# A decoder layer on one core: the place of four statistics and of the next batch's preparation

## The chip, the core and the metric

The kernel runs on 1 core of one Trainium2 chip. The metric is the device time of one execution in microseconds. Engines are named as in the profile: PE is TensorE (PEld its weight loads), DVE is VectorE, ACT is ScalarE, POOL is GpSimd, SP is SyncE. A name with a q (ACTq, SPq) is the engine's queue, which also issues DMAs.

## The reference

A post-norm decoder layer over 4 batches of 512 tokens with 512 features:

```
x = layernorm(x + linear_attention(x))               # 16 heads, chunks of 64
x = layernorm(x + expert(x, w1, w2))                 # two int8-quantised linears with a SiLU gate between
x = layernorm(x + ffn(x))

ffn:    logits = x @ gate_w.T;  top 2 of 8 experts, softmax over the two logits
        h1_e = x @ w1.T + 2 * (x @ A1_e.T) @ B1_e.T  # w1, w3: 1408 x 512; rank 16
        h3_e = x @ w3.T + 2 * (x @ A3_e.T) @ B3_e.T
        act  = silu(h1_e) * h3_e
        out  = sum over the two chosen experts of
               weight_e * (act @ w2.T + 2 * (act @ A2_e.T) @ B2_e.T)
```

float32 products are made of three matmuls of split operands (hi x hi, lo x hi, hi x lo).

## The kernel before

The first phase does attention for all batches and the expert of batch 0. The second phase (`mixture`), where the change lies, runs the feed-forward part of batch b and, beside it, the expert of batch b + 1. Each engine has its own hand-written program; they meet through semaphores only. `batches` gives the order on each: `prepare(0)`, then `hidden(b)` and `between(b)` for b = 0 and 1 in a hardware loop, then for b = 2, and for b = 3 without an expert (there is no next batch). I call the end of `hidden(b)` with `between(b)` and the start of the next `hidden` turn b; there are turns 0, 1 and 2 with an expert.

`hidden(b)` goes over 11 tiles f of 128 of the 1408 hidden features. Per tile PE forms h1 and h3 with the first choice's adapter (`first(b, f, 0)` and `first(b, f, 1)`), then adds the difference to the second choice's adapter (`second`, matmuls of L2172). ScalarE takes silu of h1 for each choice (`silu_out`, L1710). VectorE multiplies by the routing weight (`weighted`, L1905) and by h3 (`activation`, L1913), adds the two choices (L2080) and makes the low parts (`activation_lo`, L1895 and L1898) of what ScalarE has rounded (`activation_hi`). `second(b, f, 1)` overwrites h3, so it waits for `activation(b, f, 0)`. PE's `adapters_both(b, f)` follows and signals z_done.

Beside tile 10, the expert's output lies ready as a residual sum in `tokens`. VectorE takes its bn_stats (`expert_statistics`, four of L2022) before `weighted(b, 10, 0)`, and combines them (`expert_variance`, six small operations, L115 to L120) before `weighted(b, 10, 1)`.

`between(b)` has PE multiply the activations by w2: `whole_down(b, f)` for f = 0 to 8, each 4 x 3 matmuls into four banks, then tiles 9 and 10 with `adapters_out` per 128 tokens. Among these stands the preparation of batch b + 1: transposes of the tokens (`x_transposed`, L2233), `logits_across`, `logits_by_token`, `adapters_in` for U1 and U3, `masks_transposed` and `weights_spread`. A down tile comes through ScalarE's queue: `fetch_down` issues its load of 256 KB, `split_down` waits for the landing and rounds it (L1555), GpSimd's `split_down` forms the low part (L1505), and the slot is loaded again; three slots go round. `next_down(b, f)` is the split of tile f and the fetch of tile f + 2. Between them, in ScalarE's order, stand `expert_deviation` (a square root, L1674), `expert_normalise` (L1679), the store of the tokens (`store_x2`), `z_split`, `x_hi` (L1565), `masks_out` (L1580) and others. The transposes wait for the normalised tokens.

SyncE's queue loads the up weights (`f_up`, 1408 KB a tile): tile 0 of the next batch once z_done of tile 9 has come, then x3.

VectorE in `between(b)`: the shift of the expert's norm (`expert_shift`), `mask_z`, `z_split`, `x_lo`, `choose` and `weigh` (the top 2), `mask_adapters` (L1864, waits for `masks_out`), `adapters_lo`, in turns 0 and 1 `channel_top` of the expert after (L1933, two reductions over 2048 elements), and `normalise`: the residual sum of PE's outputs, its bn_stats, and the norm (L2101 to L2112). Then `hidden(b + 1)` begins on it.

Of the kernel before, what the change touches and what calls it, by code (L numbers as in the profile page):

```python
# [1246 lines left out]
def mixture(nc, shared, used, x1_dram, x2_dram, up_dram, w1, w2, down_stream, descending, out_dram):  # L1247
# [9 lines left out]
    with ExitStack() as ctx:  # L1257
# [169 lines left out]
        def tiles(b, f):  # L1427
            return b * FT + f + 1
# [114 lines left out]
        def _(sc):  # L1543
# [7 lines left out]
            def split_down(b, f):  # L1551
                r = f % DOWNS
                sc.wait_ge(down_loaded[r], PRIMED + 16 * (b * PER[r] + f // DOWNS + 1))
                sc.wait_ge(down_done, PRIMED + (tiles(b, f - DOWNS) if f >= DOWNS else b * FT))
                sc.activation(down_hi[:, r, :], down_raw[:, r, :], ACT.Copy).then_inc(down_hi_ready, 1)  # L1555

            def next_down(b, f):
                split_down(b, f)
                if f + DOWNS - 1 < FT:
                    fetch_down(b, f + DOWNS - 1)  # L1560
# [32 lines left out]
            def z_split(b):  # L1593
                sc.wait_ge(z_summed, PRIMED + b + 1)
                sc.activation(z_hi[:, :], zm[:, 2, :], ACT.Copy).then_inc(z_hi_ready, 1)
# [157 lines left out]
            def between(b, expert, another):  # L1753
                for f in range(DOWNS, 2 * DOWNS - 1):
                    fetch_down(b, f)
                if expert:
                    expert_deviation(b)
                next_down(b, 3)
                if expert:
                    expert_normalise(b)  # L1760
                    store_x2(b)
                next_down(b, 4)
                z_split(b)
                if expert:
                    x_hi(b + 1, 0)
                    x_hi(b + 1, 1)
                next_down(b, 5)
                if expert:
                    x_hi(b + 1, 2)
                    x_hi(b + 1, 3)  # L1770
                    logits_out(b + 1)
                next_down(b, 6)
                if expert:
                    softmax_exp(b + 1)
                    masks_out(b + 1)
                next_down(b, 7)
                if expert:
                    masked_hi(b + 1, 0)
                    masked_hi(b + 1, 1)
                next_down(b, 8)  # L1780
                if expert:
                    masked_hi(b + 1, 2)
                    masked_hi(b + 1, 3)
                    weights_out(b + 1)
                next_down(b, 9)
                next_down(b, 10)
                if another:
                    root(b + 1, 0)
                deviation(b)
# [4 lines left out]
        def _(dve):  # L1794
# [224 lines left out]
            def expert_statistics(b):  # L2019
                for t in range(TT):  # L2020
                    dve.wait_ge(summed, PRIMED + b * TT + t + 1)
                    dve.bn_stats(e_stats[:, t, :], xe[:, t, :]).then_inc(e_stats_ready, 1)  # L2022

            def expert_variance(b):
                dve.wait_ge(e_stats_ready, PRIMED + b * TT + TT)
                moments(dve, e_stats, e_part, e_mean[:, :], e_rstd[:, 0, :], waiter(e_moment_ready, b * 2))\
                    .then_inc(e_var_ready, 1)

            def expert_shift(b):
                dve.wait_ge(e_std_ready, PRIMED + b + 1)  # L2030
                dve.reciprocal(e_rstd[:, 2, :], e_rstd[:, 1, :]).then_inc(e_rstd_ready, 1)
                dve.wait_ge(e_rstd_ready, PRIMED + 2 * b + 1)
                dve.scalar_tensor_tensor(e_mean[:, :], e_mean[:, :], -1.0, e_rstd[:, 2, :],
                                         ALU.mult, ALU.mult).then_inc(e_rstd_ready, 1)

            def hidden(b, expert):
                for item in (WB0, WB1):
                    k, n = slot(b, item)
                    dve.wait_ge(drained[k], PRIMED + n + 1)
                for f in range(FT):  # L2040
                    if expert and f == 1:
                        scale_tokens(b, 0)
                        row_scale(b, 0, 0)
                    if expert and f == 2:
                        round_w(b, 0)
                    if expert and f == 5:
                        linear_out(b, 0)
                    if expert and f == 6:
                        channel_ratio(b, 1)
                    if expert and f == 7:  # L2050
                        scale_tokens(b, 1)
                        row_scale(b, 1, 0)
                    if expert and f == 8:
                        clamp_x(b, 1)
                    if expert and f == 10:
                        expert_statistics(b)
                    weighted(b, f, 0)
                    activation(b, f, 0)
                    if expert and f == 1:
                        row_scale(b, 0, 1)  # L2060
                    if expert and f == 2:
                        clamp_x(b, 0)
                    if expert and f == 4:
                        channel_top(b, 1, 1)
                    if expert and f == 5:
                        expert_activation(b)
                        channel_top(b, 1, 0)
                    if expert and f == 6:
                        channel_scale(b, 1)
                    if expert and f == 7:  # L2070
                        row_scale(b, 1, 1)
                        round_w(b, 1)
                    if expert and f == 9:
                        linear_out(b, 1)
                    if expert and f == 10:
                        expert_variance(b)
                    weighted(b, f, 1)
                    activation(b, f, 1)
                    dve.wait_ge(act_ready, PRIMED + 2 * tiles(b, f))
                    dve.tensor_tensor(act[:, 2, :], act[:, 0, :], act[:, 1, :], ALU.add).then_inc(sum_ready, 1)  # L2080
                    activation_lo(b, f)
# [34 lines left out]

            def between(b, expert, another):
                if expert:
                    expert_shift(b)
                mask_z(b)  # L2120
                z_split(b)
                if expert:
                    for c in range(KT):
                        x_lo(b + 1, c)
                    choose(b + 1)
                    weigh(b + 1)
                    mask_adapters(b + 1)
                    adapters_lo(b + 1)
                if another:
                    for i in range(2):  # L2130
                        channel_top(b + 1, 0, i)
                normalise(b, expert, another)
# [4 lines left out]
        def _(pe):  # L2137
# [75 lines left out]
            def whole_down(b, f):  # L2213
                for t in range(TT):
                    down(b, f, t)
# [197 lines left out]
            def between(b, expert, another):  # L2413
                whole_down(b, 0)
                whole_down(b, 1)
                adapters_second(b, FT - 1)
                adapters_both(b, FT - 1)
                whole_down(b, 2)
                if expert:
                    x_transposed(b + 1, 0)  # L2420
                    x_transposed(b + 1, 1)
                whole_down(b, 3)
                if expert:
                    x_transposed(b + 1, 2)
                    x_transposed(b + 1, 3)
                down(b, 4, 0)
                down(b, 4, 1)
                if expert:
                    logits_across(b + 1)
                down(b, 4, 2)  # L2430
                down(b, 4, 3)
                if expert:
                    logits_by_token(b + 1)
                    adapters_in(b + 1, U1)
                whole_down(b, 5)
                if expert:
                    adapters_in(b + 1, U3)
                if expert:
                    masks_transposed(b + 1)
                whole_down(b, 6)  # L2440
                if expert:
                    weights_spread(b + 1)
                whole_down(b, 7)
                whole_down(b, 8)
                for t in range(TT):
                    down(b, FT - 2, t)
                    down(b, FT - 1, t)
                    adapters_out(b, t)
                if another:
                    first_maxima(b + 1)  # L2450
# [92 lines left out]
```

## Time and profile before

| | us |
|---|---|
| three runs | 1130.33, 1132.45, 1132.54; median 1132.45 |
| profiled execution | 1128.95 |
| its span | 1127.1 |
| PE, DVE, ACT, POOL busy | 1030.8, 717.8, 402.7, 295.3 |
| mean granted clock of TensorE | 0.977 |

The span goes from the first to the last instruction. The profiled execution's own time is 1.85 us above its span. A clock of 1.00 is 2.4 GHz, 0.50 is 1.2 GHz. Recorded matmul durations overlap: from start to start a matmul of 512 columns takes less than the 0.40 us that its row shows.

### The profile page before, as it was taken

To read this page: it belongs to the slowest core of one execution; us is meant where nothing else is said; L and a number is where in the kernel's file an instruction comes from. 1 tells how busy PE (TensorE), PEld (TensorE's weight loads), DVE (VectorE), ACT (ScalarE), POOL (GpSimd) and SP (SyncE) were. 2 spreads that over 40 slices of the span, in tenths; PEclk is the share of its full clock that TensorE was granted. 3 is DMA by queue.
4 is the path that set the end of the run, shared out by engine and by line. 5 is a ranking of instruction groups with operands and counts; after the bars stand their busy time and mean duration, and the time that the engine had idled before them with its cause. 6 is when DMAs were issued, how large, how long until landed. Compare 5 with 4: busy or idle time off the path is not lost.

```text
span 1127.1 us, 13755 instructions
## 1 busy us (share of the span) xinstructions
PE 1030.8 (91%) x4920; PEld 809.6 (72%) x4920; DVE 717.8 (64%) x1150; ACT 402.7 (36%) x623; POOL 295.3 (26%) x245
## 2 busy tenths in 40 slices
PE   3799999989999827999999899999999999999997
PEld 2577777767777625777768687777777877888885
DVE  4565786785576646957657867764976774554542
ACT  3234333323342233344443253434253434322231
POOL 2247674543224400201222200142110132200021
PEclk9899999999999968999999999999999999999999
DMA  7116664130021025243463152446143327134421
GB/s 261 62 61 232 214 232 146 61 104 10 10 92 31 1 78 225 99 161 111 163 219 123 39 210 103 170 158 233 39 158 134 133 79 276 57 140 154 172 66 56
DMA packets 47862, 142.98 MB, mean 127 GB/s; under 512 B 3497, under 2 KB 14633, under 8 KB 42161
## 3 DMA queue, kind: packets, MB, share of 16 engines
q1 hardware_dynamic: 28720, 118.71, 28.8%
q10 hardware_dynamic: 19072, 23.35, 6.4%
q8 instruction: 42, 0.69, 0.3%
q14 instruction: 28, 0.22, 0.1%
HBM read 114.66 MB, written 27.39 MB: 126 GB/s over the span
## 4 chain that ended last, share of the span: by engine, by line
PE 44%; DVE 13%; issue 3%; ACT 2%; POOL 1%; DMA 1%; DVEq 0%; ACTq 0%
PE f_h L106 7%; PE f_h L107 7%; PE f_h L108 7%; PE f_h L2172 4%; PE f_y L106 3%; PE f_y L107 3%; PE f_y L108 3%; DVE f_q_mem L1933 2%; DVE f_work L1913 1%; PE f_y L2362 1%; DVE f_work L1905 1%; PE f_z_sum L106 1%; PE f_z_sum L108 1%; PE f_z_sum L107 1%; PE f_z_second L107 1%
## 5 line engine op out<-in xcount | busy, mean ns | idle before, releaser
L106 PE MATMUL f_h<-f_xT_hi,f_up 128*128 128x512 f32 x352 | 140.5, 399 | 1.6 <-issue 0.9
L107 PE MATMUL f_h<-f_xT_hi,f_up 128*128 128x512 f32 x352 | 138.4, 393 | 0.0
L108 PE MATMUL f_h<-f_xT_lo,f_up 128*128 128x512 f32 x352 | 137.7, 391 | 0.0
L106 PE MATMUL ring<-w_hi,xT_hi 128*128 128x512 f32 x256 | 110.4, 431 | 24.4 <-POOL xT_lo L429 21.8
L1505 POOL TENSOR_TENSOR f_down_lo<-f_down_raw,f_down_hi 128x512 fp32r<-128x512 f32 x44 | 61.1, 1390 | 227.5 <-ACT f_down_hi L1555 227.5
L1710 ACT ACTIVATE f_work<-f_h 128x512 f32<-128x512 f32 x88 | 52.4, 596 | 171.4 <-PE f_h L2172 114.8
L1905 DVE TENSOR_TENSOR f_work<-f_work,f_weightT 128x512 f32<-128x512 f32 x88 | 65.1, 739 | 73.7 <-ACT f_work L1710 69.9
L1516 POOL TENSOR_TENSOR weights<-weights,f_rows 128x512 f32<-128x512 f32 (+1 forms) x24 | 31.9, 1360 | 299.9 <-ACT f_rows L1637 183.6
L1913 DVE TENSOR_TENSOR f_work<-f_h,f_work 128x512 f32<-128x512 f32 x88 | 60.8, 691 | 70.8 <-PE f_h L108 65.3
L107 PE MATMUL ring<-w_hi,xT_lo 128*128 128x512 f32 x256 | 103.7, 405 | 0.0
L108 PE MATMUL ring<-w_lo,xT_hi 128*128 128x512 f32 x256 | 103.5, 404 | 0.0
L443 POOL TENSOR_TENSOR rot_b<-qk,ropes 128x256 f32<-128x256 f32 x64 | 55.8, 893 | 101.2 <-ACT qk L548 101.2
L106 PEld LDWEIGHTS ring<-w_hi,xT_hi 128*128 128x128 f32 x256 | 49.4, 193 | 41.8 <-POOL xT_lo L429 23.6
L106 PEld LDWEIGHTS f_h<-f_xT_hi,f_up 128*128 128x128 f32 x352 | 66.6, 189 | 16.9 <-issue 2.0
L108 PEld LDWEIGHTS f_h<-f_xT_lo,f_up 128*128 128x128 f32 x352 | 66.4, 189 | 14.8
L107 PEld LDWEIGHTS f_h<-f_xT_hi,f_up 128*128 128x128 f32 x352 | 66.5, 189 | 14.2
L106 PE MATMUL f_y<-f_down_hi,f_both_hi 128*128 128x512 f32 x176 | 71.9, 409 | 0.0
L107 PE MATMUL f_y<-f_down_hi,f_both_lo 128*128 128x512 f32 x176 | 70.6, 401 | 0.0
L108 PE MATMUL f_y<-f_down_lo,f_both_hi 128*128 128x512 f32 x176 | 70.5, 401 | 0.0
L2172 PE MATMUL f_h<-f_umT_hi,f_up 128*128 128x512 f32 x176 | 57.6, 408 | 13.9 <-DVE f_work L1913 13.9
L1604 ACT ACTIVATE f_second_hi<-f_work 128x512 fp32r<-128x512 f32 x44 | 27.9, 635 | 109.0 <-DVE f_work L1913 109.0
L108 PEld LDWEIGHTS ring<-w_lo,xT_hi 128*128 128x128 f32 x256 | 49.8, 195 | 12.2
(306 smaller groups left out, 2244.0 us busy)
## 6 DMA issues: line engine op xcount, KB each, us to landing
f_up<-up_scratch SPq DMA_DIRECT2D x44, 1408.0 KB, 6.2
f_down_raw<-in_down_stream ACTq DMA_DIRECT2D x44, 256.0 KB, 3.6
f_x<-x_scratch SPq DMA_DIRECT2D x7, 1024.0 KB, 8.8
scaled_w<-in_up_stream SPq DMA_DIRECT2D x6, 704.0 KB, 5.4
up_scratch<-q_mem SPq DMA_DIRECT2D x6, 704.0 KB, 3.6
up_scratch<-scaled_w SPq DMA_DIRECT2D x6, 704.0 KB, 3.1
x_tok<-in_x SPq DMA_DIRECT2D x4, 1024.0 KB, 5.6
out<-f_x SPq DMA_DIRECT2D x8, 512.0 KB, 3.1
```

What stands on the lines that cost most here:

```text
L106: pe.matmul(out, lhs_hi, rhs_hi, start=start, stop=False)
L107: pe.matmul(out, lhs_lo, rhs_hi, start=False, stop=False)
L108: return pe.matmul(out, lhs_hi, rhs_lo, start=False, stop=stop)
L443: pool.tensor_tensor(b4[:, :, :, two], q4[:, :, :, 1 - two], sin[:, :, two].unsqueeze(1).to_broadcast([P, H, DK // 2]), ALU.mult).then_inc ...
L1505: pool.tensor_tensor(down_lo[:, f % DOWNS, :], down_raw[:, f % DOWNS, :], down_hi[:, f % DOWNS, :].bitcast(F32), ALU.subtract).then_inc(do ...
L1516: pool.tensor_tensor(we[:, t, 0:C], we[:, t, 0:C], rows[:, 1, 0:C], ALU.mult).then_inc(w_scaled, 1)
L1604: sc.activation(second_hi[:, :], act[:, 1, :], ACT.Copy).then_inc(act_hi_ready, 1)
L1710: sc.activation(silu[:, choice, :], h_ps[0][:, :], ACT.Silu).then_inc(silu_ready, 1)
L1905: dve.tensor_tensor(silu[:, choice, :], silu[:, choice, :], weightT[:, choice, :], ALU.mult)\
L1913: dve.tensor_tensor(act[:, choice, :], h_ps[1][:, :], silu[:, choice, :], ALU.mult)\
L1933: dve.tensor_reduce(top[:, i, 0:C], (xe, we)[i][:, :, 0:C].rearrange("p t c -> p c t"), AX.X, ALU.max, apply_absolute_value=True).then_inc ...
L2172: last = pe.matmul(h_ps[i][:, :], weights(f, l, cols), r[:, rhs, :], start=False, stop=True, skip_group_check=True)
```

## The change

On VectorE, `expert_statistics` moves from before `weighted(b, 10, 0)` to behind `activation(b, 10, 0)`, and `expert_variance` from there to the start of `between`. On PE and ScalarE each part of the next batch's preparation moves behind one more down tile. No operation is added or taken away.

```
 ScalarE, between:
                 next_down(b, 4)
                 z_split(b)
+                next_down(b, 5)
                 if expert:
                     x_hi(b + 1, 0)
                     x_hi(b + 1, 1)
-                next_down(b, 5)
+                next_down(b, 6)
                 if expert:
                     x_hi(b + 1, 2)
                     x_hi(b + 1, 3)
                     logits_out(b + 1)
-                next_down(b, 6)
+                next_down(b, 7)
                 if expert:
                     softmax_exp(b + 1)
                     masks_out(b + 1)
-                next_down(b, 7)
+                next_down(b, 8)
                 if expert:
                     masked_hi(b + 1, 0)
                     masked_hi(b + 1, 1)
-                next_down(b, 8)
+                next_down(b, 9)
                 if expert:
                     masked_hi(b + 1, 2)
                     masked_hi(b + 1, 3)
                     weights_out(b + 1)
-                next_down(b, 9)
                 next_down(b, 10)
 VectorE, hidden:
-                    if expert and f == 10:
-                        expert_statistics(b)
                     weighted(b, f, 0)
                     activation(b, f, 0)
...
                     if expert and f == 10:
-                        expert_variance(b)
+                        expert_statistics(b)
                     weighted(b, f, 1)
                     activation(b, f, 1)
 VectorE, between:
                 if expert:
+                    expert_variance(b)
                     expert_shift(b)
 PE, between:
                 whole_down(b, 2)
+                whole_down(b, 3)
                 if expert:
                     x_transposed(b + 1, 0)
                     x_transposed(b + 1, 1)
-                whole_down(b, 3)
+                whole_down(b, 4)
                 if expert:
                     x_transposed(b + 1, 2)
                     x_transposed(b + 1, 3)
-                down(b, 4, 0)
-                down(b, 4, 1)
+                down(b, 5, 0)
+                down(b, 5, 1)
                 if expert:
                     logits_across(b + 1)
-                down(b, 4, 2)
-                down(b, 4, 3)
+                down(b, 5, 2)
+                down(b, 5, 3)
                 if expert:
                     logits_by_token(b + 1)
                     adapters_in(b + 1, U1)
-                whole_down(b, 5)
+                whole_down(b, 6)
                 if expert:
                     adapters_in(b + 1, U3)
-                if expert:
                     masks_transposed(b + 1)
-                whole_down(b, 6)
+                whole_down(b, 7)
                 if expert:
                     weights_spread(b + 1)
-                whole_down(b, 7)
                 whole_down(b, 8)
```

## Rows read from the trace of the kernel before

**Rows 1.** The page's first part: busy time, share of the span, instructions.

```profile
PE 1030.8 (91%) x4920; PEld 809.6 (72%) x4920; DVE 717.8 (64%) x1150; ACT 402.7 (36%) x623; POOL 295.3 (26%) x245
```

**Rows 2.** The chain that ended last, turn 1: start, us on the chain, engine, line.

```profile
746.04 1.86 DVE f_e_stats L2022 x3
...
783.19 1.03 ACT f_maskT L1580
```

**Rows 3.** Timeline of PE: start, us, operation, [idle before it <- who ended it].

```profile
568.17 0.74 PE L2172 MATMUL f_h<-f_umT_hi,f_up 128*128 128x512 f32 x2 [2.41 <-DVE f_work L1913]
...
633.62 0.73 PE L2172 MATMUL f_h<-f_umT_hi,f_up 128*128 128x512 f32 x2 [3.37 <-DVE f_work L1913]
...
749.26 0.73 PE L2172 MATMUL f_h<-f_umT_hi,f_up 128*128 128x512 f32 x2 [2.39 <-DVE f_work L1913]
...
811.07 0.74 PE L2172 MATMUL f_h<-f_umT_hi,f_up 128*128 128x512 f32 x2 [0.91 <-DVE f_work L1913]
...
925.98 0.73 PE L2172 MATMUL f_h<-f_umT_hi,f_up 128*128 128x512 f32 x2 [2.47 <-DVE f_work L1913]
...
938.71 1.09 PE L2233 MATMUL f_h<-ident,tokens 128*128 128x128 f32 x8 [1.26 <-ACT tokens L1679]
```

**Rows 4.** Timeline of PE: the first matmul behind down tile 1, turns 1 and 2.

```profile
757.90 0.40 PE L106 MATMUL f_z_second<-f_second_hi,f_up 128*128 128x512 f32 x1
...
933.09 0.39 PE L106 MATMUL f_z_second<-f_second_hi,f_up 128*128 128x512 f32 x1
```

**Rows 5.** Windows: length, busy PE, PEld, DVE, ACT, POOL, granted clock, DMA share, GB/s.

```profile
634.00:636.00 2.00, 2.00 (x11) 1.90 (x10) 1.38 (x3) 0.53 (x1) 0.00 (x0) 0.60 0.05 8
...
751.00:752.00 1.00, 1.00 (x4) 0.78 (x3) 0.97 (x3) 0.63 (x1) 0.00 (x0) 0.50 0.00 0
```

**Rows 6.** Timeline of DVE around the statistics of turn 1.

```profile
743.73 1.78 DVE L1898 TENSOR_TENSOR f_both_lo<-f_work,f_both_hi 128x512 fp32r<-128x512 f32 x1
745.43 2.46 DVE L2022 BATCH_NORM_STATS2 f_e_stats<-tokens 128x6 f32<-128x512 f32 x4
...
749.13 0.16 DVE L115 TENSOR_TENSOR f_e_part<-f_e_stats 128x8 f32<-128x8 f32 x1
...
749.83 0.69 DVE L1905 TENSOR_TENSOR f_work<-f_work,f_weightT 128x512 f32<-128x512 f32 x1
```

**Rows 7.** Timeline of POOL in turn 1: the low parts of down tiles 1 and 4.

```profile
744.93 1.74 POOL L1505 TENSOR_TENSOR f_down_lo<-f_down_raw,f_down_hi 128x512 fp32r<-128x512 f32 x1
...
763.51 1.30 POOL L1505 TENSOR_TENSOR f_down_lo<-f_down_raw,f_down_hi 128x512 fp32r<-128x512 f32 x1 [2.85 <-ACT f_down_hi L1555]
```

**Rows 8.** Timeline of ACT in turn 1: down tiles 3 and 4, x_hi(2) with x_hi(3).

```profile
758.66 0.63 ACT L1555 ACTIVATE f_down_hi<-f_down_raw 128x512 fp32r<-128x512 f32 x1 [3.88 <-DMA f_down_raw<-in_down_stream]
...
762.80 0.63 ACT L1555 ACTIVATE f_down_hi<-f_down_raw 128x512 fp32r<-128x512 f32 x1 [0.68 <-PE f_y L108]
...
766.72 1.18 ACT L1565 ACTIVATE f_xT_hi<-f_h 128x512 fp32r<-128x512 f32 x2 [1.28 <-PE f_h L2233]
```

**Rows 9.** DMA issues: up tile 0; down tiles 3, 6: KB each, us to landing.

```profile
f_up<-up_scratch SPq DMA_DIRECT2D x1, 1408.0 KB, 6.2
...
f_down_raw<-in_down_stream ACTq DMA_DIRECT2D x1, 256.0 KB, 6.4
...
f_down_raw<-in_down_stream ACTq DMA_DIRECT2D x1, 256.0 KB, 5.2
```

**Rows 10.** Timeline of SP's queue, turn 1: the issue of up tile 0.

```profile
751.25 0.32 SPq L1441 DMA_DIRECT2D f_up<-up_scratch  x1
```

**Rows 11.** Timeline of PE, turn 1: the first matmul of the logits.

```profile
768.69 0.40 PE L106 MATMUL f_h<-f_xT_hi,f_a_hi 128*8 128x512 f32 x1
```

**Rows 12.** Timeline of DVE: the ends of turns 1 and 2.

```profile
784.25 0.69 DVE L1864 TENSOR_TENSOR f_work<-f_z_sum,f_maskT 128x512 f32<-128x512 f32 x1 [5.53 <-ACT f_maskT L1580]
...
807.07 0.18 DVE L2110 RECIPROCAL f_rstd<-f_rstd 128x4 f32<-128x4 f32 x1 [0.27 <-ACT f_rstd L1599]
...
971.98 0.69 DVE L2101 TENSOR_TENSOR f_x<-f_y,f_x 128x512 f32<-128x512 f32 x1 [4.26 <-PE f_y L108]
```

More of the change, by code:

```diff
@@ L1763, in between @@
                 z_split(b)
+                next_down(b, 5)
                 if expert:
@@ L1766, in between @@
                     x_hi(b + 1, 1)
-                next_down(b, 5)
+                next_down(b, 6)
                 if expert:
@@ L1771, in between @@
                     logits_out(b + 1)
-                next_down(b, 6)
+                next_down(b, 7)
                 if expert:
@@ L1775, in between @@
                     masks_out(b + 1)
-                next_down(b, 7)
+                next_down(b, 8)
                 if expert:
@@ L1779, in between @@
                     masked_hi(b + 1, 1)
-                next_down(b, 8)
+                next_down(b, 9)
                 if expert:
@@ L1784, in between @@
                     weights_out(b + 1)
-                next_down(b, 9)
                 next_down(b, 10)
@@ L2054, in hidden @@
                         clamp_x(b, 1)
-                    if expert and f == 10:
-                        expert_statistics(b)
                     weighted(b, f, 0)
@@ L2075, in hidden @@
                     if expert and f == 10:
-                        expert_variance(b)
+                        expert_statistics(b)
                     weighted(b, f, 1)
@@ L2118, in between @@
                 if expert:
+                    expert_variance(b)
                     expert_shift(b)
@@ L2418, in between @@
                 whole_down(b, 2)
+                whole_down(b, 3)
                 if expert:
@@ L2421, in between @@
                     x_transposed(b + 1, 1)
-                whole_down(b, 3)
+                whole_down(b, 4)
                 if expert:
@@ L2425, in between @@
                     x_transposed(b + 1, 3)
-                down(b, 4, 0)
-                down(b, 4, 1)
+                down(b, 5, 0)
+                down(b, 5, 1)
                 if expert:
                     logits_across(b + 1)
-                down(b, 4, 2)
-                down(b, 4, 3)
+                down(b, 5, 2)
+                down(b, 5, 3)
                 if expert:
@@ L2434, in between @@
                     adapters_in(b + 1, U1)
-                whole_down(b, 5)
+                whole_down(b, 6)
                 if expert:
                     adapters_in(b + 1, U3)
-                if expert:
                     masks_transposed(b + 1)
-                whole_down(b, 6)
+                whole_down(b, 7)
                 if expert:
                     weights_spread(b + 1)
-                whole_down(b, 7)
                 whole_down(b, 8)
```

## The prediction

> **What bounds the kernel now.** I began with the page: TensorE is busy for 91% of the span [rows 1], so a change of order can only win where TensorE stands still or runs at half clock, or lose by making it do so. Next came the chain of waits and the idle times of PE around the three turns from one batch to the next (turn 0 near 568 to 634 us, turn 1 near 749 to 811, turn 2 near 926 to 986). The reader should see two kinds of place on the chain: the four bn_stats of L2022, and, at the other end of a turn, the copy of the masks (L1580) followed by VectorE [rows 2]. In the idle times the same pattern stands in every turn [rows 3]: PE waits 2.41, 2.39 and 2.47 us for VectorE's product L1913 before `second(b, 10, 1)`; in turn 2 it waits 1.26 us more for ScalarE's normalised tokens before the transposes; and at the start of the next batch it waits for VectorE again, 3.37 us in turn 0, 0.91 in turn 1.
>
> The first wait costs more than its length in turn 1 (and in turn 0, whose wait is alike). The same 30 matmuls take 8.64 us from 749.26 to 757.90 in turn 1, and 7.11 from 925.98 to 933.09 in turn 2 [rows 3, 4]. The difference, 1.5 us, is a stretch at the lower level of TensorE's clock: 0.50 granted, 1.2 GHz, behind 2.4 us without a matmul [rows 5]. Turn 2's wait of 2.47 us was followed by no such stretch in this execution. One matmul at full clock is 7.11/30, about 0.235 us, a down tile of 12 is 2.8.
>
> **Who owns the end of a turn.** In turn 1 VectorE waits 5.53 us for the masks, starts at 784.25, and then has one idle time, 0.27 us before L2110, until it hands over L1913 just ahead of 811.07 [rows 3, 12]. Everything in between (masking, `channel_top`, the last norm of this batch, then `weighted` and `activation` of the next) is queued back to back. So in turns 0 and 1 the time of the whole turn is that of the masks plus a fixed 26.8 us (811.07 less 784.25); what PE gains before is waited away at its end. Turn 2 has no `channel_top`, and there VectorE waits 4.26 us for PE's outputs at 971.98 [rows 12]: PE's own position counts.
>
> **Part 1, statistics behind the first activation.** In turn 1 VectorE ends both_lo at 745.51 (743.73 + 1.78) and does the four bn_stats (2.46 us, some 2.4 from start to start) before L1905 [rows 6]. After, L1905 comes first. But GpSimd's second `split_down` stands from 744.93 to 746.67 [rows 7], and VectorE's operations with two SBUF inputs take longer beside it: L1898 1.78 us, against 0.69 for L1905 at 749.83 with GpSimd idle [rows 6]; the bn_stats, with one such input, are not lengthened. I let L1905 finish 0.6 us behind GpSimd, at 747.3, and L1913 at 748.0. PE starts at 748.05 instead of 749.26: 1.2 us gained, 1.15 us of idle time left. Behind the waits of 0.91 and 1.26 us no stretch at 0.50 stands in this trace, so I count the 1.5 us back in turns 0 and 1. Bounds of the gain in waiting: 1.2, and 2.4 if L1905 gets in at once.
>
> The Trainium skill, page "SBUF — State Buffer", section "Who interferes with whom", says that a VectorE instruction with two SBUF inputs and a GpSimd instruction that reads SBUF exclude each other, whoever issues first holding the ports for its whole length. GpSimd's row starts first here, which by that rule gives the 1.2; had VectorE been first, it would be 2.4.
>
> Behind it the statistics lie in front of `weighted(b, 10, 1)`. From 748.0 they take 2.4, so L1905 starts at 750.3 rather than 749.83 [rows 6]: 0.5 us late, although the six small variance operations (0.7 us, 749.13 to 749.83) have gone. Queued behind are activation, sum, both lows, and ScalarE's `activation_hi`, after which it issues the loads of down tiles 3 and 4: 0.5 us later each. PE itself has two down tiles to do before it wants these lows, 5.6 us of cover. `expert_variance` in `between` ends near 754.6, hidden by ScalarE's wait for down tile 3 until 758.66 [rows 8]; without that cover it would cost its 0.7 us.
>
> **Part 2, one down tile earlier than the preparation.** No instruction is added or removed on PE, ScalarE or the DMA queues; GpSimd's and SyncE's order stays. But the masks now stand behind one more down tile, +2.8 us, so the masks come earlier only if PE gained more than that. PE gained 2.7 in turns 0 and 1 (shift at best about +0.1) and 1.2 plus the 1.26 of the transposes in turn 2 (about +0.3).
>
> The real limit is another chain, from the landing L of down tile 3 (758.66 in turn 1 [rows 8]). ScalarE splits it, normalises, issues the store and gets to tile 4 at L + 4.14, as before; GpSimd has its low at L + 6.15 (763.51 + 1.30) [rows 7, 8]. PE now needs that low before tile 4, ahead of transposes 2 and 3: L + 6.15 + 2.8 + 0.95 + 1.4 = L + 11.3 for the logits matmuls. And ScalarE now splits tile 6 before x_hi(2). Tile 6 is fetched at L + 4.2 behind the 1 MB store and needs 5.2 us [rows 9]: L + 9.4. Half a microsecond of split, then the 1.97 us from x_hi(2) to the logits (766.72 to 768.69) [rows 8, 11]: L + 11.9. Before, the logits started at L + 10.0, right behind the down matmuls. So the masks shift by 1.85 plus the shift of L.
>
> L: `f_up` of 1408 KB is issued at 751.25 and needs 6.2 us, so it lands near 757.4; the 256 KB of down tile 3 need 6.4 and land 1.2 behind it [rows 8 to 10], so I read them as held up by it. `f_up` waits for z_done of tile 9, right behind the wait that shrinks, hence 1.2 us earlier. I take L 1.2 us earlier. Bounds: 0.5 later (its own issue) and 2.4 earlier. The masks then come 1.85 - 1.2 = 0.65 us later than now.
>
> The Trainium skill, page "DMA: Bandwidth & Descriptors", section "Queues, rings and completion order", says that each DMA engine goes round robin between queues, packet by packet. A tile on ScalarE's queue should then not stand behind SyncE's, and its landing would follow its own issue, 0.5 later, which is the slow rival below; the 6.4 us speak against an even share.
>
> **The sum.** Turn 0: +0.65. Turn 1: +0.65, and now PE arrives 2.15 earlier at the end of the turn (2.8 less 0.65), so its 0.91 us of waiting becomes 0.91 + 2.15 + 0.65 = 3.7 us, and behind 3.37 the clock fell in turn 0 [rows 5]: +1.5. Turn 2: 0.65 - 2.8 = -2.15, kept by PE. Together 3 x 0.65 + 1.5 - 2.8 = +0.65 us. The profiled execution took 1128.95 us (span 1127.1 and 1.85 around it), 3.5 less than the median of 1132.45; a difference carries over, so 1133.1. The last batch has no preparation behind it and changes nothing.
>
> **Rivals.** (a) The low clock in turn 1 stays away: -0.85, 1131.6. Speaks for it: turn 2's 2.47 us without one. (b) L1905 isn't held by GpSimd: PE's first wait closes, `f_up` starts 2.4 earlier, the masks shift by 1.85 - 2.4 = -0.55; 3 x -0.55 - 1.3 = -2.95, 1129.5. Against it: [rows 6, 7]. (c) Slower: down tile 3 lands 0.5 later, with its issue; shift 2.35, 3 x 2.35 - 1.3 = +5.75, 1138.2. It decides once the shift passes 1.2, that is, once L moves less than 0.65 forward. (d) VectorE doesn't set the end of turns 0 and 1, the shift reaches PE as in turn 2: 3 x -2.15 = -6.45, 1126.0. Against it: 26 us without a gap. (e) Turn 2's wait is followed by a low clock in most other executions, so that the runs win 1.5 there which this trace hides: -0.85, 1131.6.
>
> **Chances.** The forecast 45%, (a) and (e) 25% together, (b) 10%, (c) 13%, (d) 5%, 2% else. Changes under 0.2%, 2.3 us, can't be told from none. Forecast, (a) and (e) lie inside, with an error of about 1.5 us each, giving some 56% same; (b), (d) and the low tails 23% faster; (c) and the high tails 21% slower. The range runs from (b) to just short of (c): 1129.5 to 1137.5.
>
> **What will show it.** PE's wait before `second(b, 10, 1)` about 1.15 us and no 0.50 clock behind it; L1905 there 1.3 to 1.8 us long; down tile 3 landing about 1.2 us earlier against the wait's end kept in place; gaps of some tenths of a microsecond before down tiles 3 and 4 and the logits; VectorE's start on the masks 0.65 later within the turn; PE's wait at the end of turn 1 above 3 us with a 0.50 clock; turn 2 alone about 2 us shorter. I am wrong if the first wait closes, or the masks come earlier than now, or VectorE has idle time behind them.

## The result: slower by 0.46%, and where it went

The changed kernel takes 1137.1 us (median of 6 runs, 1135.36 to 1138.27) against 1132.38 for the kernel before (6 runs): ratio 1.0046, 95% interval 1.0033 to 1.0058. I had forecast 1133.1 and no measurable change. 1137.1 lies inside my range, 1129.5 to 1137.5, but only because the range ended just short of the slow rival (c), and (c) is what happened. The profiled execution took 1135.39 us, its span is 1133.6.

The page's first part, of the kernel after:

```profile
PE 1030.5 (91%) x4911; PEld 809.6 (71%) x4920; DVE 723.6 (64%) x1150; ACT 402.6 (36%) x623; POOL 297.1 (26%) x245
```

PE has the same work as in [rows 1] (nine matmul records are missing from this trace); the time is idle time. The timeline of PE after, at the places of [rows 3] and at new ones (start, us, operation, idle time before it and who ended it):

```profile
568.87 0.73 PE L2171 MATMUL f_h<-f_umT_hi,f_up 128*128 128x512 f32 x2 [1.13 <-DVE f_work L1913]
582.13 0.49 PE L106 MATMUL f_y<-f_down_hi,f_both_hi 128*128 128x512 f32 x1 [1.79 <-POOL f_down_lo L1505]
...
626.26 0.79 PE L106 MATMUL f_h<-f_xT_hi,f_up 128*128 128x512 f32 x1 [3.19 <-issue]
...
637.81 0.72 PE L2171 MATMUL f_h<-f_umT_hi,f_up 128*128 128x512 f32 x2 [2.16 <-DVE f_work L1913]
...
752.11 0.73 PE L2171 MATMUL f_h<-f_umT_hi,f_up 128*128 128x512 f32 x2 [1.14 <-DVE f_work L1913]
765.09 0.49 PE L106 MATMUL f_y<-f_down_hi,f_both_hi 128*128 128x512 f32 x1 [1.53 <-POOL f_down_lo L1505]
769.24 0.50 PE L106 MATMUL f_y<-f_down_hi,f_both_hi 128*128 128x512 f32 x1 [0.22 <-POOL f_down_lo L1505]
774.96 0.40 PE L106 MATMUL f_h<-f_xT_hi,f_a_hi 128*8 128x512 f32 x1 [0.40 <-DVE f_xT_lo L1810]
815.20 0.74 PE L2171 MATMUL f_h<-f_umT_hi,f_up 128*128 128x512 f32 x2 [2.28 <-ACT f_work L1710]
817.27 1.20 PE L2171 MATMUL f_h<-f_umT_hi,f_up 128*128 128x512 f32 x2 [1.10 <-DVE f_work L1913]
...
931.58 0.73 PE L2171 MATMUL f_h<-f_umT_hi,f_up 128*128 128x512 f32 x2 [1.21 <-DVE f_work L1913]
```

The first wait of each turn has fallen to 1.13 to 1.21 us, as worked out. New are the waits for the low part of down tile 3 (1.79, 1.53 and, in turn 2, 1.53 us), of tile 4 (0.22) and for the logits (0.40). At the end of turn 1 PE now waits 3.4 us (2.28 and 1.10) instead of 0.91, and at the end of turn 0 3.19 and 2.16 us instead of 0.88 and 3.37.

Executions differ by up to 4.4 us before the first turn, where all kernels here run the same code, so I compare lengths inside the second phase and not spans. The marks are rows of PE: the transposes of the quantised activations ahead of turn 0 (541.63 before, 543.61 after), the transposes of the channel maxima in the batch that follows (694.39 and 698.50; then 871.06 and 877.93), and the second-choice matmuls behind turn 2 (985.90 and 992.32). Differences of neighbours, and the start of the copy of the masks counted from the same mark ahead of turn 1 (722.73 and 726.84):

| | turn 0 | turn 1 | turn 2 | masks of turn 1 |
|---|---|---|---|---|
| before | 152.76 | 176.67 | 114.84 | 60.46 |
| after | 154.89 | 179.43 | 114.39 | 62.60 |
| difference | +2.13 | +2.76 | -0.45 | +2.14 |

The sum is +4.44 us; the other 2 us between the two spans arose before turn 0. Counted the same way, the masks come 2.37 us later in turn 0 and 2.35 in turn 2. The low clock behind the first wait of turn 1 is gone (1.00, where before there was 0.50 [rows 5]), and one has come at the end of the turn. In turn 0 the kernel before has two low stretches (from 569.5 and 634.4), the kernel after one (from 626.2, at the end of the wait of 3.19). Windows of the kernel after, columns as in [rows 5]:

```profile
753.00:755.00 2.00, 2.00 (x10) 1.60 (x9) 2.00 (x4) 0.00 (x0) 0.00 (x0) 1.00 0.32 56
...
817.00:819.00 2.00, 1.73 (x5) 1.45 (x6) 0.81 (x3) 0.00 (x0) 0.00 (x0) 0.58 0.60 226
```

Timelines of SyncE's and ScalarE's queues and of ScalarE after, and the issue of down tile 3 with its us to landing (the last line):

```profile
753.80 0.32 SPq L1441 DMA_DIRECT2D f_up<-up_scratch  x1
754.32 0.39 SPq L1445 DMA_DIRECT2D f_x<-x_scratch  x1
...
756.69 0.34 ACTq L1547 DMA_DIRECT2D f_down_raw<-in_down_stream  x1
...
763.06 0.63 ACT L1555 ACTIVATE f_down_hi<-f_down_raw 128x512 fp32r<-128x512 f32 x1 [3.15 <-DMA f_down_raw<-in_down_stream]
...
f_down_raw<-in_down_stream ACTq DMA_DIRECT2D x1, 256.0 KB, 6.3
```

From the mark, `f_up` is now issued 1.56 us earlier (26.96 instead of 28.52; [rows 10]), as the forecast wanted. But down tile 3 is split at 36.22 instead of 35.93 [rows 8]: 0.29 us later (0.50 in turn 0, 0.48 in turn 2). It did not move with `f_up`. And VectorE's queue behind the masks is as long as before, here its two idle times (timeline of DVE after; compare [rows 12]):

```profile
790.49 0.69 DVE L1864 TENSOR_TENSOR f_work<-f_z_sum,f_maskT 128x512 f32<-128x512 f32 x1 [5.51 <-ACT f_maskT L1580]
813.26 0.18 DVE L2108 RECIPROCAL f_rstd<-f_rstd 128x4 f32<-128x4 f32 x1 [0.27 <-ACT f_rstd L1599]
```

790.49 to 817.27 is 26.78 us, against 26.82 before. Turn 0 is different, which I had overlooked: there the stretch lasts 30.42 us before (603.20 to 633.62) and 30.26 after, because VectorE stands idle inside it. Timeline of DVE, the first product of the next batch, first in the kernel before, then after:

```profile
632.15 0.69 DVE L1905 TENSOR_TENSOR f_work<-f_work,f_weightT 128x512 f32<-128x512 f32 x1 [3.69 <-issue]
```

```profile
636.34 0.69 DVE L1905 TENSOR_TENSOR f_work<-f_work,f_weightT 128x512 f32<-128x512 f32 x1 [3.60 <-ACT f_work L1710]
```

In the kernel before, the silu that it reads had ended at 628.21. The same idle time of 3.56 to 3.69 us stands in every kernel here, and only at the end of turn 0, where the programs step back to the start of the hardware loop; at the end of turn 1, where they leave it, there is none (L1905 starts at 809.60, behind an operation that ends at 809.49). The DMA view of the kernel before lists two packets of kind instruction between 629 and 634 us and none between 803 and 812. That points to the loading of instructions, but no run here tests it.

### The profile page after: what moved, and what is told of

Same layout as the page of the kernel before. It is cut to its first block, busy times and chain, and to the rows that moved or that the text cites. A ratio compares the mean times of both kernels' runs of the same rounds, so it can differ in the third digit from the quotient of the medians.

```text
span 1133.6 us, 13746 instructions
## 1 busy us (share of the span) xinstructions
PE 1030.5 (91%) x4911; PEld 809.6 (71%) x4920; DVE 723.6 (64%) x1150; ACT 402.6 (36%) x623; POOL 297.1 (26%) x245
## 4 chain that ended last, share of the span: by engine, by line
PE 42%; DVE 12%; DMA 3%; issue 3%; ACT 3%; POOL 1%; ACTq 0%; DVEq 0%
PE f_h L106 7%; PE f_h L107 7%; PE f_h L108 7%; PE f_h L2171 4%; DMA f_down_raw<-in_down_stream 3%; PE f_y L106 2%; PE f_y L108 2%; PE f_y L107 2%; DVE f_work L1905 2%; DVE f_work L1913 1%; PE f_y L2361 1%; DVE f_q_mem L1933 1%; PE f_z_sum L106 1%; PE f_z_sum L107 1%; PE f_z_sum L108 1%
## 5 line engine op out<-in xcount | busy, mean ns | idle before, releaser
L1905 DVE TENSOR_TENSOR f_work<-f_work,f_weightT 128x512 f32<-128x512 f32 x88 | 69.2, 787 | 73.6 <-ACT f_work L1710 73.5
```

What stands on the lines that cost most here:

```text
L1905: dve.tensor_tensor(silu[:, choice, :], silu[:, choice, :], weightT[:, choice, :], ALU.mult)\
```

## The experiments

Each was run on the same chip as the kernel before, whose medians in the three groups were 1132.83, 1132.22 and 1132.92. Turn lengths come from the same marks.

**1 and 2: each part alone.** e1 has part 1 on the order of before, e2 part 2 with the statistics left in place; their diffs are the two halves of the diff shown.

> The order of before, with the statistics alone moved behind the first activation (and the variance into between). Theory T (the landing of down tile 3 paces a turn): PE's first wait falls from 2.4 to 1.15 us, but the load of tile 3 is issued 0.5 later and lands 0.3 to 0.5 later, and the transposes wait for it (normalised tokens at landing + 3.5), so PE idles some 3 us before them instead of 0 to 1.3. Each turn 0.3 to 0.5 longer, 1133.3 to 1134; up to 1.5 a turn more if that idle time brings the low clock. Rival R (PE's first wait is what costs): 1.2 us a turn gained and 1.5 of clock in turns 0 and 1, about 1126.

> The statistics and the variance where they were, the preparation one down tile later. Theory T: down tile 3 lands as in the kernel before; the masks come 2.4 us later in turns 0 and 1 and both turns lengthen by that, turn 2 shortens by about 0.9: 1136.4. Rival R (the later order is free and hides the 1.26 us before the transposes): 1131 to 1132.4.

e1: 1138.53 us, ratio 1.0038 (1.0024 to 1.0052). Turns 155.45, 177.16, 118.08. e2: 1136.7 us, ratio 1.0038 (1.0023 to 1.0052). Turns 153.86, 180.62, 114.83. Both parts lose alone, and together they lose about as much as either. PE of e1, timeline:

```profile
753.86 0.74 PE L2171 MATMUL f_h<-f_umT_hi,f_up 128*128 128x512 f32 x2 [1.13 <-DVE f_work L1913]
768.72 1.06 PE L2232 MATMUL f_h<-ident,tokens 128*128 128x128 f32 x8 [3.39 <-ACT tokens L1679]
...
945.69 1.97 PE L2232 MATMUL f_h<-ident,tokens 128*128 128x128 f32 x8 [3.17 <-ACT tokens L1679]
```

The wait taken away at 753.86 has gone to the transposes. From its mark (728.60) they stand at 40.12, against 39.64 in the kernel before: 0.48 us later, as much as the landing of down tile 3, whose load is issued 0.37 later (29.84 from the mark instead of 29.47). Turn 1 grew by 0.49. The rest of the loss goes with the low clock: from 944.7 on the record shows 6.8 us at 0.50 in turn 2, which is 3.2 us longer, and turn 0 (2.7 us longer) has a stretch behind its wait of 3.53 and one of 6.8 us at its end. Rival R (1126) falls. In e2 the load is issued as before (29.46 from the mark), but `f_up` only 0.52 us ahead of it instead of 0.95, and it lands 0.80 later; the masks of turn 1 come 2.65 us later than before and the turn is 3.95 longer, low clock at its end included. Turn 2 has a low stretch that the profile before lacks (from 934.7) and gains nothing instead of 0.9. T gave 1136.4.

**3: the loads beside down tile 3, held back.**

```
                     sp.wait_ge(z_done, PRIMED + tiles(b, FT - 2))
+                    sp.wait_ge(down_loaded[0], PRIMED + 16 * (b * len(range(0, FT, DOWNS)) + 2))
                     load_up(0)
```

> The changed kernel, in which SyncE's queue issues up tile 0 and x3 of the next batch only when down tile 3 has landed. If f_up and x3 on the other queue slow down tile 3, it lands 2.6 to 3.5 us behind its issue instead of 6.4, the waits for the lows of tiles 3 and 4 go, and the turns shorten by 0.9 to 2.5 each (tile 6 and the store now run beside f_up): 1130 to 1134.5. If the 6.4 us are not from sharing: 1137, tile 3 as late as now.

1144.64 us, ratio 1.0094 (1.0077 to 1.0112). DMA issues of down tiles 3 and 6 (us to landing), and ScalarE's timeline at tile 6:

```profile
f_down_raw<-in_down_stream ACTq DMA_DIRECT2D x1, 256.0 KB, 2.7
...
f_down_raw<-in_down_stream ACTq DMA_DIRECT2D x1, 256.0 KB, 10.3
...
779.17 0.63 ACT L1556 ACTIVATE f_down_hi<-f_down_raw 128x512 fp32r<-128x512 f32 x1 [5.38 <-DMA f_down_raw<-in_down_stream]
```

Half the expectation held: alone, down tile 3 lands 2.7 us behind its issue instead of 6.3, so the rest is sharing. The time was missed by 10 us, since the two loads now run beside the store and tiles 5 and 6. Tile 6 takes 10.3 us, x_hi(2) is queued behind its split in the new order, and PE waits 3.4 to 4.6 us before the logits. The place in ScalarE's order for which I had counted 0.6 us costs whatever that load costs.

**4: the split of tile 6 behind x_hi(3).**

```
-                next_down(b, 6)
                 if expert:
                     x_hi(b + 1, 2)
                     x_hi(b + 1, 3)
+                next_down(b, 6)
+                if expert:
                     logits_out(b + 1)
```

> The changed kernel with ScalarE's split of down tile 6 moved from before x_hi(2) to behind x_hi(3). Theory T: the wait of 0.38 to 0.45 us before the logits goes, the masks come 0.4 earlier in each turn: 1135.9. If the split of tile 6 is not what the logits wait for: 1137.1 and the wait stays.

1137.3 us, ratio 1.0033 (1.0021 to 1.0044); the changed kernel had 1.0046, so the times don't tell them apart. The wait before the logits fell from 0.38 and 0.40 to 0.18 us in turns 0 and 1: tile 6 was what they waited for, but it is worth 0.2 us and not the 0.4 expected. This execution had two low stretches more (766.8 in turn 1, 947.7 in turn 2) and a longer one at the end of turn 1 (818.0), which cover anything of that size.

**5 and 9: the two loads behind the transposes.** On e1. e5 moves both, e9 only x3.

```
-                    sp.wait_ge(z_done, PRIMED + tiles(b, FT - 2))
-                    load_up(0)
-                    sp.wait_ge(summed, PRIMED + TT * (b + 1))
-                    load_x3(x2_dram[bass.ts(b, T), :])
                     tokens_transposed(b + 1)
                     if another:
                         sp.wait_ge(x2_stored, PRIMED + 16 * (b + 2))
                         load_expert_tokens(b + 1)
+                    sp.wait_ge(z_done, PRIMED + tiles(b, FT - 2))
+                    load_up(0)
+                    sp.wait_ge(summed, PRIMED + TT * (b + 1))
+                    load_x3(x2_dram[bass.ts(b, T), :])
```

> The statistics moved, the preparation where it was, and SyncE's loads of up tile 0 and of x3 for the next batch issued behind the transposes and the expert's tokens. If the landing of down tile 3 beside those two loads is what paces a turn: it lands 2.7 us behind its issue, the wait of 3.2 to 3.5 us before the transposes (statistics alone) goes, the masks come 2.7 us earlier than in the kernel before, and every turn is some 2.5 us shorter: 1125 to 1128. If it isn't: as the statistics alone, 1138.

> Statistics moved, preparation where it was; of SyncE's two loads only x3 is issued late (behind the transposes), up tile 0 stays early. Theory X (down tile 3 shares the DMA engines with f_up and then with x3, and lands only when x3 has nearly landed): without x3 it lands 3 to 4.5 us behind its issue, PE's wait before the transposes falls from 3.3 to about 1 or less, 1124 to 1127. The reading of the prediction (down tile 3 is held by f_up alone): x3 makes no difference, still 6.3 us, 1138.

e5: 1122.89 us, 2 us below the range expected, ratio 0.9916 (0.9903 to 0.9929); turns 149.66, 173.75, 112.09; the wait before the transposes is gone in every turn. e9: 1124.7 us, ratio 0.9937 (0.9919 to 0.9954); turns 150.11, 174.38, 112.73. Down tile 3 of e5 (us to landing); then of e9 `f_up`, down tile 3 and PE's wait for the tokens in turn 1:

```profile
f_down_raw<-in_down_stream ACTq DMA_DIRECT2D x1, 256.0 KB, 2.6
```

```profile
f_up<-up_scratch SPq DMA_DIRECT2D x1, 1408.0 KB, 6.0
...
f_down_raw<-in_down_stream ACTq DMA_DIRECT2D x1, 256.0 KB, 3.8
...
759.05 1.06 PE L2232 MATMUL f_h<-ident,tokens 128*128 128x128 f32 x8 [0.60 <-ACT tokens L1679]
```

With `f_up` still early, the load of 256 KB takes 3.8 us, with both loads early 6.5 (e1). Of the 3.9 us that the two loads add to the 2.6 of e5, the larger part, 2.7, comes from x3, 1 MB behind `f_up` on the same queue.

**6 and 7: who owns the end of a turn.** The two reductions of `channel_top` move ahead of the masks, on the kernel after (e6) and before (e7). The second line keeps the transposes of the maxima waiting for both.

```
                     for c in range(KT):
                         x_lo(b + 1, c)
+                    if another:
+                        channel_top(b + 1, 0, 1)
                     choose(b + 1)
                     weigh(b + 1)
+                    if another:
+                        channel_top(b + 1, 0, 0)
                     mask_adapters(b + 1)
                     adapters_lo(b + 1)
-                if another:
-                    for i in range(2):
-                        channel_top(b + 1, 0, i)
...
-                    pe.wait_ge(top_ready, PRIMED + 4 * b + i + 1)
+                    pe.wait_ge(top_ready, PRIMED + 4 * b + 2)
```

> The changed kernel with the two reductions of channel_top (7.6 us of VectorE) moved into idle times of VectorE ahead of the masks. Theory V (VectorE's queue behind the masks sets the end of turns 0 and 1): PE's waits at the end of both turns go and PE's own position counts, turn 0 about 5 us shorter than in the kernel before, turn 1 about 1, turn 2 as in the changed kernel: 1125 to 1127. Rival d of the prediction (VectorE does not set the end): 1137 as the changed kernel.

> The kernel before with the same move of channel_top. Theory V: turn 0 4.9 us shorter (3.4 of wait, 1.5 of clock), turn 1 0.75, turn 2 the same: 1127. Against it the changed kernel with this move should then be about 1 us faster instead of 4.7 slower, since its 0.5 to 0.6 us a turn of PE position is no longer lost. Rival d: 1132.8.

e6: 1129.13 us, ratio 0.9966 (0.9954 to 0.9979); turns 151.16, 176.67, 115.76. e7: 1131.38 us, ratio 0.9986 (0.9976 to 0.9997); turns 151.75, 176.27, 116.06. DVE and PE of e6, timelines; then DVE of e7 at the end of turn 0:

```profile
796.17 0.69 DVE L2099 TENSOR_TENSOR f_x<-f_y,f_x 128x512 f32<-128x512 f32 x1 [1.37 <-PE f_y L108]
...
810.99 0.73 PE L2172 MATMUL f_h<-f_umT_hi,f_up 128*128 128x512 f32 x2 [0.16 <-DVE f_work L1913]
```

```profile
633.93 0.69 DVE L1905 TENSOR_TENSOR f_work<-f_work,f_weightT 128x512 f32<-128x512 f32 x1 [3.59 <-ACT f_work L1710]
```

V holds in kind: VectorE now waits for PE, PE's 3.4 us at the end of turn 1 have become 0.16 (with 1.40 us at 823.47, a tile later), and the changed kernel goes from 0.46% slower to 0.34% faster than before, although its masks come 2.70 us late. Once that queue is gone the change no longer costs: e6 lies 2 us under e7, with intervals that overlap by 0.0003. V's sizes were too large: I had counted turn 0 at 4.9 to 5 us, and it gave 1.0 (e7) and 1.6 (e6). VectorE's idle time at the loop's step is still there in both, so PE still waits behind it: 2.52 us in e7, with a low stretch behind, 2.12 in e6, with none.

**8 and 12: the causes taken away together.** e8 is e5 with the move of `channel_top`. e12 adds one wait on GpSimd, before its second split of a batch with an expert.

```
                 for f in range(DOWNS):
+                    if expert and f == 1:
+                        pool.wait_ge(act_ready, PRIMED + 2 * tiles(b, FT - 1) - 1)
                     split_down(b, f)
```

> Statistics moved, preparation where it was, up tile 0 and x3 loaded late, channel_top in VectorE's idle times. Both causes removed: turn 0 shorter by 7, turn 1 by 3.4, turn 2 by 2.5: 1119 to 1121. If the late loads and the end of a turn overlap in what they win, 1124.

> The fastest kernel so far (statistics moved, both loads late, channel_top in idle times), and GpSimd waits for the activation of tile 10's first choice before its second split. If GpSimd's split is what makes L1905 take 1.8 us there, L1905 takes 0.7, PE's wait of 1.13 us before the second-choice matmuls goes, and each turn is 1.1 us shorter: 1117.3. If L1905 is long for another reason, 1120.7 and the wait stays.

e8: 1120.72 us, ratio 0.9896 (0.9883 to 0.9910); turns 147.97, 173.86, 112.06. e12: 1116.89 us, ratio 0.9874 (0.9855 to 0.9894); turns 146.80, 172.02, 110.98. L1905 in front of the statistics, timelines of DVE: first the kernel after, then e12 with the bn_stats behind it.

```profile
749.54 1.79 DVE L1905 TENSOR_TENSOR f_work<-f_work,f_weightT 128x512 f32<-128x512 f32 x1
```

```profile
741.17 0.68 DVE L1907 TENSOR_TENSOR f_work<-f_work,f_weightT 128x512 f32<-128x512 f32 x1
...
742.49 2.46 DVE L2024 BATCH_NORM_STATS2 f_e_stats<-tokens 128x6 f32<-128x512 f32 x4
```

1.79 us beside GpSimd, 0.68 without it, and PE's wait before the second-choice matmuls no longer appears: the forecast of part 1 by GpSimd's rows was right, and every turn is 1.1 to 1.8 us shorter than in e8. This is what the Trainium skill, page "SBUF — State Buffer", section "Who interferes with whom", says of VectorE instructions with two SBUF inputs beside GpSimd.

**10 and 11: late loads with the whole change, and alone.** The diff of e5 on the kernel after and on the kernel before.

> The whole change with both loads late. With down tile 3 early the masks are limited by PE alone: one down tile more (2.8) against the 1.2 and 1.5 gained, so the masks come as in the kernel before and 2.5 later than without the later preparation. Turns 0 and 1 unchanged to the kernel before, turn 2 2.5 shorter: 1130. If the later preparation costs nothing where down tile 3 is early: 1123.

> The kernel before with both loads late and nothing else. There down tile 3 lands early too, but PE reaches the transposes only 0.1 us before the tokens are ready in turns 0 and 1, so nothing is won there; turn 2 loses its 1.26 us of waiting: 1131. If the loads are worth more by themselves than that, the 9 us of the two together belong mostly to them: 1125.

e10: 1127.98 us, ratio 0.9963 (0.9954 to 0.9972); turns 151.50, 177.94, 112.01. e11: 1129.12 us, ratio 0.9968 (0.9954 to 0.9982); turns 152.03, 175.47, 114.86. Both came 2 us below their figures. Late loads win 0.32% alone and the moved statistics lose 0.38% alone, but the two together win 0.84%: the statistics' gain is real and had been held back by down tile 3. The later preparation costs on top of it: 0.84% faster without, 0.37% with it; with it, the intervals don't tell the kernel from the late loads alone. In e10 the masks of turn 1 stand at 60.16 from the mark, in e5 at 57.51: 2.65 us, a down tile less a little.

## Why the prediction was wrong

**The step that failed** is "I take L 1.2 us earlier", resting on the reading that `f_up` holds the load of down tile 3, which lands 1.2 us behind it. In turn 1 `f_up` moved 1.56 us forward and the landing moved 0.29 back. x3 follows `f_up` on SyncE's queue; I had left it out of the argument. With x3 away and `f_up` in place the load takes 3.8 us (e9), with both away 2.6 to 2.7. But the load does not wait for the end of either: x3 was issued 1.56 us earlier as well, and down tile 3 lands 1.2 us behind `f_up` and 2.9 ahead of x3 in the kernel before, 2.8 behind and 1.1 ahead in the kernel after. What stayed is the distance to its own issue, 6.4 and 6.3 us (7.2 in e2, where `f_up` starts just ahead of it). How the transfers share the time within it no run resolves. The load's issue is late because the statistics now stand in front of `weighted(b, 10, 1)`: +0.38 with them there, +0.37 in e1, none in e2. A landing that comes later with its issue is rival (c), which I gave 13% and 1138.2. The 6.4 us were no evidence against it. The Trainium skill, page "DMA: Bandwidth & Descriptors", section "Queues, rings and completion order", says that the DMA engines go round robin between queues; that the landing followed its own issue agrees with it.

**With L right most of the rest of the sum holds.** The masks' shift by that formula is 1.85 plus that of L: 2.35, 2.14 and 2.33 us in the three turns, 2.37, 2.14 and 2.35 measured; in e2 it is 1.85 + 0.80 = 2.65, 2.65 measured. Turns 0 and 1: the masks' shift passed through to the end, as +2.13 of 2.37 and as the larger part of +2.76. Over the kernels where no low stretch at the end of turn 1 came or went, turn 1 moved as its masks did: e1 +0.45 and +0.49, e5 -2.95 and -2.92, e9 -2.32 and -2.29 us. e11 is an exception, -1.88 and -1.20: a wait of PE of 1.29 us at 822.87, behind the stretch, came there and was not followed up. Turn 2: 2.35 - 2.8 = -0.45, measured -0.45.

**A second reading was wrong, at little cost here.** That "in turns 0 and 1 the time of the whole turn is that of the masks plus a fixed 26.8 us" was read from turn 1 alone. In turn 0 it is 30.42 us, 3.69 of them an idle time of VectorE that I took for queued work. It is the same in both kernels, so the difference between them hardly notices it; it spoiled the sizes that I expected of e6 and e7.

**Part 1.** The wait fell by 1.25 us in turn 1 (1.2 forecast), L1905 took 1.79, the load was issued 0.38 later (0.5 forecast). The clock stayed up behind it, in turn 0 too. All of that was right, and none of it reached the end in turns 0 and 1. **Part 2**: the new waits for tiles 3, 4 and the logits are those worked out (0.22 and 0.40), except tile 3's, 1.53 instead of some tenths, because of L.

**The clock.** I charged 1.5 us for the low clock at the end of turn 1. It came (817.4), and the turn is 0.6 us longer than its masks explain. A low stretch is paid only in part where a wait behind it gets shorter; the kernel before had 0.79 us of waiting at 832.91 that has gone. How often each execution has which stretch stays open; over the profiles here turn 2's wait of 2.47 us was followed by a low stretch in e2, e7 and e11, and not in the kernel before. Rival (e) is thus neither shown nor refuted, and a difference of 1.5 us between single profiles can be the clock's alone.

**Rivals (b) and (d)** fell: L1905 was held by GpSimd (e12), and VectorE sets the end of turns 0 and 1 (e6, e7), in turn 0 with its idle time included.

## What to carry to other kernels

A transfer that lands late is not explained by the largest neighbour alone: list everything in flight until it lands, and ask of each whether it is needed soon; two loads that could wait cost more here than the whole edit was about (x3 is issued at 751.77 in the kernel before and first used at 798.82). Before moving work off a wait, follow the engine that releases the *end* of the stage, since a gain ahead of a queue without gaps is waited away, and a delay of its first operation is not. An edit that loses may still hold a gain: the moved statistics lose 0.38% alone, and with the two loads late they turn 0.32% into 0.84%. The later preparation held none. And read each turn's rows by themselves: the same code had 3.6 us of idle time in the loop and none behind it.

## What the runs showed of the hardware

The 256 KB of a down tile landed in 2.6 to 2.7 us with the other queue quiet, 3.8 beside 1.4 MB, 6.3 to 6.5 beside 1.4 MB and 1 MB (7.2 in e2), and 10.3 behind a 1 MB store with those two running. Four kernels (before, e2, e7, e11) have PE's first wait of a turn at 2.39 to 2.47 us: 8 of these 12 waits were followed by a low stretch. Nine have it at 1.13 to 1.21 us, and none of the 27 was. The low stretches lasted 3.4 or 6.8 us in the records; one of 6.8 in e1 came with 3.2 us more for turn 2.
